# Shifted rows for the FFN moved tile by tile into one of two buffers, and both halves of the q sums on GpSimd

## The reference

```python
def shift_tokens(t):
    a, s = jnp.split(t, 2, -1)
    s = jnp.pad(s, ((0, 0), (1, 0), (0, 0)))[:, :-1]
    return jnp.concatenate([a, s], -1)
...
def attn_layer(x, Wqkv, qs, ksc, Wo):          # 16 heads of 64, windows of 32 that look one window back
    q, k, v = jnp.split(x @ Wqkv, 3, -1)
    ...
    q = l2norm(q) * qs
    k = l2norm(k) * ksc
    q = q * cos * scale + rotate_half(q) * sin * scale
    k = k * cos * inv + rotate_half(k) * sin * inv
    ...
def ffn_layer(x, g, bln, W1, b1, W2, b2):
    xn = (x - mu) / jnp.sqrt(var + 1e-05) * g + bln
    a, gate = jnp.split(xn @ W1 + b1, 2, -1)
    return a * jax.nn.gelu(gate, approximate=False) @ W2 + b2
for i in range(DEPTH):                         # DEPTH = 6
    x = attn_layer(shift_tokens(x), ...) + x
    x = ffn_layer(shift_tokens(x), ...) + x
```

## Time and profile before

| | |
|---|---|
| time, median of 3 runs | 2215.2 us (2207.94 to 2216.47) |
| profiled execution, its own time | 2216.56 us |
| span of the profiled execution | 2214.5 us |
| mean granted TensorE clock | 0.938 |
| busy in the span: PE, PEld, DVE, ACT, POOL | 1898.6, 1306.2, 1528.6, 1293.0, 1472.5 us |

### The profile page before, as it was taken

One profiled execution on the slowest core, in us unless ns is written; L12 is line 12 of the kernel. 1 busy time (PEld: TensorE's weight loads), 2 busy tenths in 40 slices (PEclk: granted clock), 3 DMA queues, 4 the chain that ended last, 5 costly groups with the idle time before them and its releaser, 6 DMA issues.

```text
span 2214.5 us, 61533 instructions
## 1 busy us (share of the span) xinstructions
PE 1898.6 (86%) x24771; PEld 1306.2 (59%) x24771; DVE 1528.6 (69%) x2364; ACT 1293.0 (58%) x1860; POOL 1472.5 (66%) x2112
## 2 busy tenths in 40 slices
PE   5789999968789988899889888898889888898885
PEld 2455555545566666566666566566666666566663
DVE  2445454458777787787777867787677876787872
ACT  3567777535556655565656655565556655565552
POOL 3344444458778677787777867787677776787771
PEclk8899999988999999999999999999899998999998
DMA  4999999920020000110000200002000020000000
GB/s 122 307 349 355 340 360 345 323 58 9 11 60 11 11 13 11 47 23 11 12 11 21 52 11 12 11 10 62 10 11 13 10 61 11 12 10 12 13 9 22
DMA packets 109618, 175.05 MB, mean 79 GB/s; under 512 B 49517, under 2 KB 72985, under 8 KB 108569
## 3 DMA queue, kind: packets, MB, share of 16 engines
q1 hardware_dynamic: 109336, 171.11, 24.9%
HBM read 87.06 MB, written 68.29 MB: 70 GB/s over the span
## 4 chain that ended last, share of the span: by engine, by line
PE 33%; DVE 17%; issue 11%; DMA 11%; POOL 4%; ACT 2%; SPq 1%; DVEq 0%; POOLq 0%; ACTq 0%
DMA behind<-x 10%; DVE turned L703 7%; PE yps L610 6%; PE ring L594 6%; PE ring L629 6%; PE ring L580 5%; PE ring L535 4%; PE ring L545 4%; DVE rsum L739 2%; DVE smax L724 2%; DVE pT L752 2%; DVE ss L718 1%; ACT squares L378 1%; POOL roped L328 1%; DVE stats L768 1%
## 5 line engine op out<-in xcount | busy, mean ns | idle before, releaser
L703 DVE TENSOR_TENSOR turned<-ring,ropes 128x1024 f32<-128x1024 f32 x384 | 447.5, 1207 | 20.4 <-PE ring L535 19.8
L610 PEld LDWEIGHTS yps<-wvo,oT 128*128 128x128 f32 x3072 | 398.4, 207 | 53.2 <-issue 50.0
L610 PE MATMUL yps<-wvo,oT 128*128 128x128 f32 x3072 | 405.6, 289 | 2.8 <-issue 2.1
L535 PE MATMUL ring<-wqk,xT 128*128 128x512 f32 x768 | 368.2, 602 | 7.7 <-issue 3.7
L328 POOL TENSOR_TENSOR roped<-roped,rnorm 128x1024 f32<-128x1024 f32 x192 | 362.3, 1902 | 7.5
L244 POOL TENSOR_TENSOR roped<-turned 128x512 f32<-128x512 f32 x288 | 357.5, 1271 | 13.3 <-DVE turned L703 13.3
L378 ACT ACTIVATE squares<-ring 128x1024 f32<-128x1024 f32 x192 | 197.5, 1029 | 268.8 <-DVE turned L703 268.0
L545 PE MATMUL ring<-ident,roped 128*128 128x128 f32 x1536 | 218.6, 292 | 146.0 <-ACT squares L378 128.7
L1233 POOL TENSOR_SCALAR less<-less,lowest 128x512 f32<-128x512 f32 x256 | 174.4, 693 | 241.1 <-DVE lowest L1202 241.1
L545 PEld LDWEIGHTS ring<-ident,roped 128*128 128x128 f32 x1536 | 187.9, 151 | 224.3 <-POOL roped L328 159.8
L1202 DVE CUSTOM_DVE_ANT_0 less<-ps_b,shifted 128x512 f32<-128x512 f32 x256 | 166.6, 689 | 222.4 <-PE ps_b L1065 80.0
(11 more groups left out here) (136 smaller groups left out, 3017.4 us busy)
## 6 DMA issues: line engine op xcount, KB each, us to landing
shifted<-scratch_w SPq DMA_DIRECT2D x64, 1024.0 KB, 12.7
scratch_w<-wrows SPq DMA_DIRECT2D x48, 1026.0 KB, 11.0
scratch_w<-x SPq DMA_DIRECT2D x16, 1026.0 KB, 10.3
wqk<-in_l_wqkv SPq DMA_DIRECT2D x6, 1024.0 KB, 5.4
xs<-xs SPq DMA_DIRECT2D x96, 48.0 KB, 1.9
wv<-in_l_wqkv SPq DMA_DIRECT2D x6, 512.0 KB
wo<-in_l_wo SPq DMA_DIRECT2D x24, 128.0 KB
xs<-x SPq DMA_DIRECT2D x96, 32.0 KB
```

The lines of the kernel that those rows point to most:

```text
L535: last = nc.tensor.matmul(out[:, half, :], xT[:, t % SEQT * P:(t % SEQT + 1) * P], wqk[:, layer_of(t), at + half * 512:at + (half + 1) * 5 ...
L610: last = nc.tensor.matmul(out[:, 0:D], oT[:, h, :], wvo[:, layer_of(t), r, j, :], start=h == 0, stop=h == HEADS - 1)
L703: ins = nc.vector.tensor_tensor(turned[:, n, part, :].rearrange("p (h d) -> p h d", d=DH), heads, table, ALU.mult)
```

## The change

Three edits.

- `shift` is called with a tile and not a group. In each period `n`, SP issues for tile `n-3` the single row that comes from the tile before (none for a group's first tile), waits for that tile's `add_y`, and issues the transfer of 127 rows of this one tile. The last 3 tiles are shifted behind the loop. A group thus has 7 transfers where it had 2, of as many bytes in all.
- `behind` has two buffers, used by even and odd groups, and `halves_of` reads the one of its group. A transfer waits for the normalisation of the group before the last (`xn_made`), as its buffer is then free. The memset of the first row covers both.
- `POOL_HALVES, DVE_HALVES` become `(0, 1), ()`: GpSimd makes both halves of the q sums, VectorE none.

```diff
-        behind = sb("behind", [P, SEQT, D // 2])
+        behind = sb("behind", [P, 2, SEQT, D // 2])
...
-        OWN, PREV, LOADS, BEHIND = 3 * 16, 2 * 16, 10 * 16, 2 * 16
+        OWN, PREV, LOADS, BEHIND = 3 * 16, 2 * 16, 10 * 16, (2 * SEQT - 1) * 16
...
-            return x[:, g % BATCH * SEQT + tile, 0:half], behind[:, tile, :]
+            return x[:, g % BATCH * SEQT + tile, 0:half], behind[:, g % 2, tile, :]
...
-            def shift(g):
-
-                at, half = g % BATCH * SEQT, D // 2
-                sp.wait_ge(s["y_added"], SEQT * (g + 1))
-                at_least(sp, s["xn_made"], g)
-                sp.dma_start(behind[1:P, :, :], x[0:P - 1, at:at + SEQT, half:D]).then_inc(s["behind_in"], 16)
-                sp.dma_start(behind[0:1, 1:SEQT, :], x[P - 1:P, at:at + SEQT - 1, half:D]).then_inc(s["behind_in"], 16)
+            def shift(t):
+
+                if live(t):
+                    at, tile, half, p = t % TILES, t % SEQT, D // 2, t // SEQT % 2
+                    at_least(sp, s["xn_made"], t // SEQT - 1)
+                    if tile > 0:
+                        sp.dma_start(behind[0:1, p, tile, :], x[P - 1:P, at - 1, half:D]).then_inc(s["behind_in"], 16)
+                    sp.wait_ge(s["y_added"], t + 1)
+                    sp.dma_start(behind[1:P, p, tile, :], x[0:P - 1, at, half:D]).then_inc(s["behind_in"], 16)
...
             for n in range(NT):
                 windows(n)
-                if n % SEQT == 2 and n >= SEQT:
-                    shift(n // SEQT - 1)
+                shift(n - 3)
...
-            for g in range(GROUPS - 1, GROUPS):
-                shift(g)
+            for t in range(NT - 3, NT):
+                shift(t)
...
-        POOL_HALVES, DVE_HALVES = (0,), (1,)
+        POOL_HALVES, DVE_HALVES = (0, 1), ()
```

## The result

The changed kernel takes 2044.7 us (median of 4 runs, 2042.4 to 2052.5) against 2214.1 in the same comparison: a ratio of 0.9245, 95% interval 0.9214 to 0.9276. The profiled execution has 2045.3 us, a span of 2043.5 and a granted clock of 0.977 instead of 0.938. The forecast was 2087, its range 2030 to 2140; the time lies inside, 42 us under the point. It lies also under the 2055 to 2133 of the forecast's main case, 11 us above the 2034 of its rival of a hidden sum; what this says of the mechanism is taken up behind the experiments.

A forecast was written before the change was run, and what follows sets the result against it. The transfer wait of DVE's statistics bounded the kernel; without it POOL would, at 62.2 us a group plus 2.2 of layer work, 64.4 against 69.8: 2216.6 - 24 x (69.8 - 64.4) = 2087 us, range 2030 to 2140.

The forecast's parts named there:

- the forecast's main case: Whole kernel: POOL's pace with what PE adds once a layer, 2055 to 2133 us, chance 0.60.
- rival of a hidden sum: POOL's added sum and PE's extra work overlap wholly, leaving POOL's floor of 62.2 us a group: 2034 us, chance 0.15.
- The transfer: Shifted rows before DVE's statistics: a tile's pieces land within 2.6 to 3.6 us, remaining wait taken as 0.
- The rival of a late transfer: Landing does not follow the number of pieces; DVE's statistics still wait 7.2 us a group: 2260 us, chance 0.05.
- the estimate from the Trainium skill: Transfer of shifted rows: fixed 2.0 us plus bytes over 436 GB/s, so splitting would gain 0.2 us.
- The clock and the stretch of step 3: Stretch around the statistics falls from 23.7 to about 16 us; granted clock behind them is 1.00.
- The five further issues and the second buffer at 0: SP's queue: extra issues each group cost nothing thanks to slack, and the second buffer's removed wait gains nothing here.
- POOL sets the pace: POOL's tile becomes 14.77 us with the fourth sum, 62.2 us a group, above the other links.
- The other links: The pipeline's links besides POOL, once the transfer wait and slow clock go: 61.6 us a group.
- the forecast's 64.4: Time per group: POOL's 62.2 us plus 2.2 for PE's work once a layer.
- The stretches of step 2 grow to near 14.8: A sign of the forecast: step 2's stretches of a group grow from 13.1 us to near 14.8.
- The rival with the sums wholly on top: The wait is won back without the clock and every added POOL sum stands on the path: 2164 us, chance 0.13.

The follow-up runs named there:

- the transfers alone: Changed kernel with VectorE keeping the second half of the q sum, so only the transfers by tile and two buffers: 2029.5 us, 0.9174; run again 2028.8 us.
- the fifth sum: Changed kernel with one more 128x512 sum on POOL in each tile, into a tile nobody reads: 2117.3 us, 0.9566.
- e5_join_early: Transfers by tile, with VectorE's half of the q sum made ahead of the sums of squares and not behind them: 2073.8 us, 0.9363.
- e7_filler_two: Changed kernel with an unused 128x512 sum of two SBUF inputs on VectorE, where its q sum had been: 2066.0 us, 0.9342.
- e8_filler_one: Changed kernel with an unused 128x512 reduction of one SBUF input on VectorE, in that same place: 2046.6 us, 0.9247.

## Why the prediction was right, and where its size was off

**The transfer: right.** The wait went from 171.9 to 3.7 us, for the reason given: of a group's pieces only a quarter now follows the last `add_y`. The landing took 3.7 us, a little above the 2.6 to 3.6. The remaining wait was bounded by 0 to 0.7 and taken as 0: it is 0.83 us in the group shown of the transfers alone, and nothing in the changed kernel up to its last group, since `add_y` no longer stands behind VectorE's sum. The rival of a late transfer is out. So is the estimate from the Trainium skill ("DMA: Bandwidth & Descriptors"), whose fit is of transfers that GpSimd issues, where SP issues these: 10.4 us for the group and 3.7 for a tile, against its 2.3 and 2.1. Seven transfers issued together land after 10.0, hardly sooner than two.

**The clock and the stretch of step 3: right.** 15.91 us in the group shown, against "about 16", at a clock of 1.00.

**The five further issues and the second buffer at 0: right.** One buffer gives 2046.0, and in the changed kernel's profile no engine waits for a transfer into `xs`.

**POOL sets the pace: right for three stretches of four, mis-sized.** The step of the sum that failed is the length of POOL's tile: "13.53 + 1.24 = 14.77", beside the sentence that VectorE's side of the sums "is worth nothing of its own". The 13.53 was read from a kernel in which VectorE's sum held POOL's clamp for 0.30 us in each tile. The edit that adds 1.24 us to POOL also removes that hold, so the tile measures 14.43. With it, four tiles, b2, the deviations and the rope tables are 57.7 + 2.5 + 0.6 = 60.9 us a group, and with the 2.2 us of layer work 63.1; the profile has 62.9. That POOL's length is on the path is shown by the fifth sum, not by busy time. By busy time the forecast's own sign against it, that PE rather than POOL is seldom idle, was met (95% and 89%); it does not tell the two apart. The margin is thin, too. The other links were put at 61.6 us a group, and the transfers alone take 62.1.

In numbers, over the 95 tiles between the first and the last maximum the forecast's 64.4 is 36 us more than was measured. The other 6 or 7 us lie outside of these: there the two kernels differ by 8 us, (2214.5 - 1656.8) - (2043.5 - 1493.8), where the forecast had some 1.3. Of these 8, 5.3 lie behind the last maximum (53.1 us before, 47.8 changed) and belong to the transfers: the last group's wait there fell from 10.3 us to 3.7. Every run with the early issue has 46 to 48 us there, and every run without it 53 to 54. The other 2.6 lie ahead of the first maximum, in a part that the change does not touch and that differs by more than that between runs (the first maximum of the changed kernel came at 501.9 and, run again, at 510.5).

**"The stretches of step 2 grow to near 14.8": wrong.** They stayed at 13.2 in the group shown. One reading fits, though no run tests it by itself: POOL enters step 2 with what step 1 gave back, so a lack of 1.3 us against the rest does not show there but in step 0.

**The rivals.** Wholly hidden sums were to give POOL's floor, 2034. The time came near it, but not for that reason: the floor itself was 1.3 us a group too high, and with the measured tile it is 2216.6 - 24 x (69.8 - 60.9) = 2003. Nor is the sum hidden wholly: a fifth sum costs 73 us of its 102, and one less gains 15 to 33. That is little beside the 86 us (96 x 0.90) by which POOL's tiles are shorter without it, so most of the fourth sum does lie beside the other links. The rival with the sums wholly on top, 2164, is out.

## What to carry to other kernels

- When a transfer made of many small pieces stands behind the last of several producers, issue each producer's part when it is ready. Here the number of pieces left behind the last one set the wait, and cutting the transfer without issuing it earlier gained almost nothing. Look also whether the pieces land one after the other, as with 127 rows, or together, as with 128.
- An engine's time per tile, read from a trace, holds what its neighbours do to it. Before adding work to it, look whether its short instructions come in two lengths, and what runs beside the longer ones.
- Two edits of one change want two runs. Here one gains 0.4% alone and costs 0.7 to 1.6% beside the other, since the other leaves POOL the engine that is waited for.

## What the runs showed of the hardware

VectorE and GpSimd slow each other when both make sums of two tensors in SBUF: 128x512 took 1.28 us and not 0.70 on VectorE, and three such sums some 0.4 us more on GpSimd (e5_join_early); a 128x32 clamp on GpSimd took 0.51 instead of 0.21 us beside such a sum (the kernel before), or a GpSimd sum 1.73 instead of 1.27 (e7_filler_two), and the clamp 0.21 beside a reduction with one input (e8_filler_one). The Trainium skill ("GPSIMD Engine Reference", Key points) states contention between the two engines for VectorE's instructions with two SBUF inputs; the runs agree: a reduction with one input left GpSimd at 0.21 us. The forecast did not use this rule, and its size hung on it.

Of SP's transfers within SBUF, pieces of 256 bytes from 127 rows went one after the other, one every 16 ns (the 508 pieces of a group were in after 10.4 us), and those of 128 rows nearly all at once (the DMA share was 0.72 and not 0.08).
